# Residual stack of four layers: gating cut in two around the turns of x, low-rank transpose between the two chunk products

## The reference, cut to what matters

```
x = x + L0(x)   # masked long convolution per sequence h, kernel from 64 complex states: irfft(rfft(u) * rfft(k)), plus u * D
x = x + L1(x)   # x @ W1.T + 2 * sum over 8 experts of gate * (x @ A_e.T) @ B_e.T, 16 ranks each
                # gate: softmax of the top 2 of (x @ Wr.T + language bias)
x = x + L2(x)   # x @ W2.T + 0.5 * (x @ A_labeler) @ B.T, 32 ranks, A chosen by the label of the row
x = x + L3(x)   # x @ w_eff.T, w_eff quantized by a codebook, plus a low-rank delta
```

## Time and profile before

| what | value |
|---|---|
| median of 3 runs | 1117.43 us |
| the profiled execution | 1117.58 us, of it span 1115.8 us |
| PE busy | 1028.8 us (92% of the span) |
| PE weight load busy | 811.9 us (73%) |
| DVE busy | 851.0 us (76%) |
| ACT busy | 427.3 us (38%) |
| POOL busy | 286.8 us (26%) |
| HBM | 67 GB/s over the span |

### The profile page before, as it was taken

The page is one execution under the profiler, slowest core; times in us unless marked ns, Lnnn a source line. Parts: engine busy times, 40 slices in busy tenths (PEclk is TensorE's granted clock), DMA queues, the critical chain, the costliest instruction groups (busy, mean ns, idle before and its releaser), DMA issues.

```text
span 1115.8 us, 16634 instructions
## 1 busy us (share of the span) xinstructions
PE 1028.8 (92%) x4851; PEld 811.9 (73%) x4851; DVE 851.0 (76%) x1679; ACT 427.3 (38%) x851; POOL 286.8 (26%) x318
## 2 busy tenths in 40 slices
PE   3999999999979489999999999999999999999997
PEld 2545556988868378787788778877887788778785
DVE  5797988898970568877887788778877787778762
ACT  3222222222454344354434444444444444544431
POOL 1200340374342422321132113211321123112200
PEclk9999999999989689999999999999999999999999
DMA  9501010100003244534454445434543454344311
GB/s 249 146 20 57 19 38 1 38 1 1 1 1 50 36 69 87 99 69 76 81 99 73 73 81 100 76 69 82 100 79 66 85 96 83 66 85 89 71 38 38
DMA packets 317019, 74.95 MB, mean 67 GB/s; under 512 B 292979, under 2 KB 309555, under 8 KB 316987
## 3 DMA queue, kind: packets, MB, share of 16 engines
q1 hardware_dynamic: 316986, 74.56, 34.1%
HBM read 57.61 MB, written 16.91 MB: 67 GB/s over the span
## 4 chain that ended last, share of the span: by engine, by line
DVE 27%; issue 15%; PE 13%; ACT 9%; DVEq 1%; SPq 1%; ACTq 1%; DMA 0%
DVE ZZ L1388 7%; ACT SK L1251 5%; DVE ZZ L1379 5%; PE bank L1114 4%; DVE xT L1399 3%; PE bank L1142 3%; DVE Sl L1393 3%; PE bank L1123 2%; DVE xT L1353 2%; ACT xh L1221 2%; ACT O L1284 1%; PE bank L1169 1%; DVE low L1448 1%; PE bank L1132 1%; PE bank L1158 1%
## 5 line engine op out<-in xcount | busy, mean ns | idle before, releaser
L1068 POOL TENSOR_TENSOR Cl<-QC,Ch 128x256 fp32r<-128x256 f32 x32 | 29.7, 928 | 517.6 <-ACT Ch L1233 517.6
L1142 PE MATMUL bank<-Mh,x0l 128*128 128x512 f32 x512 | 160.9, 396 | 0.0
L1142 PE MATMUL bank<-Ml,x0h 128*128 128x512 f32 x512 | 160.5, 395 | 0.0
L1142 PE MATMUL bank<-Mh,x0h 128*128 128x512 f32 x512 | 160.3, 394 | 0.0
L1251 ACT ACTIVATE SK<-ZZ 64x448 f32<-64x448 f32 x128 | 73.8, 577 | 207.2 <-DVE ZZ L1388 204.8
L530 PE MATMUL bank<-E,A 128*128 128x512 f32 (+1 forms) x384 | 129.8, 499 | 0.0
L1388 DVE SCALAR_TENSOR_TENSOR ZZ<-ZZ,coef 128x192 f32<-128x192 f32 (+1 forms) x256 | 121.8, 516 | 10.1 <-DVE ZZ L1379 0.2
L1142 PEld LDWEIGHTS bank<-Mh,x0l 128*128 128x128 f32 x512 | 96.2, 188 | 22.9
L1142 PEld LDWEIGHTS bank<-Ml,x0h 128*128 128x128 f32 x512 | 96.2, 188 | 22.6
L530 PEld LDWEIGHTS bank<-E,A 128*128 128x128 f32 x384 | 65.6, 197 | 64.0 <-issue 64.0
L1142 PEld LDWEIGHTS bank<-Mh,x0h 128*128 128x128 f32 x512 | 94.6, 188 | 18.5
(11 more groups left out here) (283 smaller groups left out, 2022.9 us busy)
## 6 DMA issues: line engine op xcount, KB each, us to landing
X<-in_x SPq DMA_DIRECT2D x256, 64.0 KB, 2.4
XT<-in_x SPq DMA_DIRECT2D x256, 64.0 KB, 2.3
out_x<-O SPq DMA_DIRECT2D x64, 256.0 KB, 3.2
toep<-kpad SPq DMA_DIRECT2D x128, 64.0 KB, 2.2
E<-in_L_cond_W SPq DMA_DIRECT2D x8, 512.0 KB, 6.7
W2s<-in_L_cond_W SPq DMA_DIRECT2D x8, 512.0 KB, 4.3
vq<-in_L_cond_weight SPq DMA_DIRECT2D x8, 512.0 KB, 3.4
LA<-in_L_cond_lora_A SPq DMA_DIRECT2D x8, 80.0 KB, 3.4
```

Source lines behind the costliest of these rows:

```text
L1142: pe.matmul(psO[nh][:, :], xs[:, c, :], ms[:, c, nh * BANK:(nh + 1) * BANK], start=(c == 0 and n == 0), stop=False)
```

## The change

Three edits, one on each of three engines:

- VectorE: `gate` is cut in two. The first part (logits, top 2, gap, indices) stays where it was; the second part (all that needs the exponential) comes behind the two turns `turn_T(i+1)`.
- ScalarE: `gate_exp(i)` stands between the state copies of the first head and those of the second, instead of behind all copies and `s_hi`. `b_hi(i+3)` comes behind `low_hi(i)`.
- TensorE: `state_transpose(i+3)` moves from behind `gated_transpose(i)` to behind `low_transpose(i)`, and both stand between `within(i+2, 0)` and `within(i+2, 1)`.

```
--- before.py
+++ after.py
@@ -1177,16 +1177,17 @@
                         chunk_states(i + 2, 1)
                     main(i, range(NC // 2, NC))
                     gated_transpose(i)
-                    if next3:
-                        state_transpose(i + 3)
                     if next1:
                         from_states(i + 1, 0)
                         from_states(i + 1, 1)
                     low_gated(i)
                     gated_out(i)
-                    low_transpose(i)
                     if next2:
                         within(i + 2, 0)
+                    low_transpose(i)
+                    if next3:
+                        state_transpose(i + 3)
+                    if next2:
                         within(i + 2, 1)
                     low_out(i)
 
@@ -1242,11 +1243,11 @@
                             act.activation(ZZ[hh * N:(hh + 1) * N, :, ri, :], psZ[hh][ri * N:(ri + 1) * N, 0:SB].rearrange("p (c b) -> p c b", b=B),
                                            ACT.Copy).then_inc(z_out, 1)
 
-                def states_out(i, first=False):
+                def states_out(i, heads, first=False):
                     act.wait_ge(scan_step, SCAN_STEPS * (i + 1))
                     if not first:
                         act.wait_ge(sl_done, i)
-                    for hh in range(HB):
+                    for hh in heads:
                         for ri in range(2):
                             act.activation(SK[ri * N:(ri + 1) * N, hh, :].rearrange("p (c b) -> p c b", b=B), ZZ[hh * N:(hh + 1) * N, :, ri, :],
                                            ACT.Copy).then_inc(sk_done, 1)
@@ -1291,18 +1292,20 @@
                             x_hi(i + 2, hh)
                     if next1:
                         c_hi(i + 1)
-                        states_out(i + 1)
+                        states_out(i + 1, (0,))
+                    gate_exp(i)
+                    if next1:
+                        states_out(i + 1, (1,))
                         s_hi(i + 1)
-                    gate_exp(i)
                     if next2:
                         states_in(i + 2)
                     gated_hi(i)
                     if next1:
                         x0_hi(i + 1, 0)
                         x0_hi(i + 1, 1)
+                    low_hi(i)
                     if next3:
                         b_hi(i + 3)
-                    low_hi(i)
 
 
                 act.sem_inc(out_taken, 1)
@@ -1314,7 +1317,7 @@
                 for hh in range(HB):
                     x_hi(1, hh)
                 b_hi(1)
-                states_out(0, first=True)
+                states_out(0, range(HB), first=True)
                 s_hi(0, first=True)
                 x0_hi(0, 0)
                 x0_hi(0, 1)
@@ -1404,11 +1407,11 @@
                     cols = slice(hh * B, (hh + 1) * B)
                     dve.tensor_tensor(x0l[:, :, cols], xT[:, :, cols], x0h[:, :, cols].bitcast(F32), ALU.subtract).then_inc(x0l_done, 1)
 
-                GATE_STEPS = 10
-
-                def gate(i):
-
-                    done = [0]
+                GATE_STEPS, GATE_EARLY = 10, 4
+
+                def gate(i, part):
+
+                    done = [(0, GATE_EARLY)[part]]
 
                     def step(ins):
                         done[0] += 1
@@ -1417,13 +1420,16 @@
 
                     logit, top, gap, e, g0, g1, g = (gsm[:, k, :] for k in range(7))
                     w = gsm[:, 7, :]
-                    dve.wait_ge(lr_done, i + 1)
-                    step(dve.tensor_tensor(logit, psL[:, ER:ER + E], langbias[:, :], ALU.add))
-                    hold(dve, "dve")
-                    step(dve.max(top, logit))
-                    dve.tensor_tensor(gap[:, 0:1], top[:, 1:2], top[:, 0:1], ALU.subtract).then_inc(gap_done, 1)
-                    step(dve.max_index(gidx[:, :], top, logit))
-                    step(dve.tensor_copy(top[:, 0:2], gidx[:, 0:2]))
+                    if part == 0:
+                        dve.wait_ge(lr_done, i + 1)
+                        step(dve.tensor_tensor(logit, psL[:, ER:ER + E], langbias[:, :], ALU.add))
+                        hold(dve, "dve")
+                        step(dve.max(top, logit))
+                        dve.tensor_tensor(gap[:, 0:1], top[:, 1:2], top[:, 0:1], ALU.subtract).then_inc(gap_done, 1)
+                        step(dve.max_index(gidx[:, :], top, logit))
+                        step(dve.tensor_copy(top[:, 0:2], gidx[:, 0:2]))
+                        assert done[0] == GATE_EARLY
+                        return
                     dve.wait_ge(gexp_done, i + 1)
                     step(dve.tensor_scalar(w[:, 2:3], e[:, 0:1], 1.0, None, ALU.add))
                     step(dve.reciprocal(w[:, 0:1], w[:, 2:3]))
@@ -1479,10 +1485,12 @@
                         carry_across(i + 1, 2)
                         carry(i + 1, 3)
                         carry_across(i + 1, 3)
-                    gate(i)
+                    gate(i, 0)
                     if next1:
                         turn_T(i + 1, 0)
                         turn_T(i + 1, 1)
+                    gate(i, 1)
+                    if next1:
                         s_lo(i + 1)
                     gated_lo(i)
                     if next1:
```

## The result

The changed kernel takes 1075.24 us (median of 4 runs, 1073.91 to 1076.87) against 1116.66 us (4 runs of the kernel before beside it): ratio 0.963, 95% interval 0.961 to 0.965. Forecast were 1078.0, and 1073 to 1088 as the range. The profiled execution took 1073.91 us, its span 1072.1.

The account below looks back on a forecast made before the run. TensorE was taken as the bound, with holes from waits. Tiles of 21.14 instead of 22.46 save 1.32 us 28 times, 37.0, plus 2.6 in the first: 1117.58 − 39.6 = 1078.0 us, range 1073 to 1088.

Parts of the forecast that it names:

- The hole before `from_states`: On TensorE, 1.08 us a tile lost waiting for VectorE's Sl; claimed to close whole.
- the margin of Sl: VectorE's Sl, done 1.18 us after the gated transpose, would be done about 1.2 us before it.
- The surplus buys nothing: Sl done 2.48 us earlier closes the 1.08 us hole before `from_states`; being earlier than needed gains nothing more.
- The hole before the low-rank transpose: On TensorE, 0.28 us a tile between the last `gated_out` pair and L1158; claimed to close too.
- G to O: TensorE, start of gated transpose (L1147) to start of `low_out` (L1169): 6.32 us before, forecast 5.0.
- the lower end: G to O of 4.87 us, set by VectorE reaching low_lo only after x0l; time 1074.4 us.
- O to the next G: TensorE, start of `low_out` to the next gated transpose: 16.14 us, nothing waits there, taken as unchanged.
- by TensorE alone 4.96: G to O from TensorE's work only: 6.32 less the holes of 1.08 and 0.28 us.
- The exposed low-rank chain: Rival: `low_out` waits for ScalarE's lowTs, G to O 5.30, 1086.4 us; chance 0.14.
- The wait for hgTl: Rival: ScalarE's queue runs late, `low_gated` waits and half the gain goes, 1098 us; chance 0.05.
- the lower clock: Rival: TensorE's granted clock falls in the loop; 50 us of work at the lower level give 1128; chance 0.04.
- transposes that cost more than 0.11 each: Rival: state transposes cost the skill page's about 275 ns each, `low_out` at G+5.29, 1086 us; chance 0.02.

Follow-up runs that it names:

- states_only: Also cited as 3: kernel before, with only the state transposes moved behind the first chunk product and b_hi behind low_hi; 1117.39 us, ratio 1.001.
- 6: Whole change, but the second part of the gating stands ahead of the turns again, exponential still early; 1074.52 us, ratio 0.963 to the kernel before.
- 5: Whole change, but the exponential stands again behind all state copies and Sh; 1084.17 us, ratio 0.971 to the kernel before.
- lolo_early: As lolo_swap, with the low-rank transpose between second and third product of the first chunk product; 1070.73 us, ratio 0.958 to the kernel before.
- lolo_swap: Whole change, but VectorE's low_lo stands ahead of the low part of x of the second head; 1077.52 us, ratio 0.965 to the kernel before.
- 2: Kernel before, with TensorE's new order alone and b_hi behind low_hi, gating and exponential as before; 1125.77 us, ratio 1.009.
- 8: Whole change, but the low-rank transpose stands ahead of both chunk products; 1083.60 us, ratio 0.970 to the kernel before.
- 1: Kernel before, with the edits on VectorE and ScalarE alone, TensorE in its old order; 1083.69 us, ratio 0.971.

## Why the prediction was right

**Size.** Forecast was a tile of 21.14 and a gain of 37.0 us in 28 tiles plus 2.6 in the first. Measured are 21.12 a tile, 38.4 us in the 28 tiles (the kernel before takes 22.48 in the mean, not 22.46) and 2.1 in the first, where `from_states` keeps 0.3 us of its hole. From the first gated transpose to the last, the kernel before takes 693.01 us (413.02 to 1106.03) and the one after 652.52 (409.82 to 1062.34): 40.5 us. The other 3.2 us by which the two profiled spans differ stand ahead of the first gated transpose; in `states_only`, whose gating is that of the kernel before, it also comes early (410.66), so most of this is probably the execution and not the change.

**The hole before `from_states`.** Right: it closes whole, VectorE waits for hgTh instead, and the margin of Sl is 0.96 us (1.2 forecast). The difference is the 0.28 us by which VectorE's turn of x now starts later behind low_lo; from the CAST's end to Sl's end it takes 4.26 us, as forecast (4.21). "The surplus buys nothing" holds for the split (6): either order of turns and gating does. It does not hold for the exponential (5): without its early place the two engines meet with nothing to spare, and 0.22 us a tile return.

**The hole before the low-rank transpose, and `low_out`.** Right in sum, mis-sized in its parts: G to O is 4.87, the lower end, not 5.0; O to the next G is 16.24, not 16.14. The two errors cancel, and that the tile came out within 0.02 us is luck. `low_out` starts right behind low_lo, its weights can't be loaded before, and its pair keeps TensorE 0.57 us instead of 0.48. So 0.1 to 0.2 us a tile are still a wait for VectorE; `lolo_early` shows it, whose tiles are 0.15 shorter. The term "by TensorE alone 4.96" was too large: without a wait TensorE reaches `low_out` at +4.78 (`lolo_swap`). The sum had left in the low-rank transpose at the 0.29 us that it took behind its wait (643.45 to 645.12, less six products of 0.23), and it takes 0.11 without one (625.09 to 625.20).

**What the prediction missed.** It took TensorE for the bound and its waits for holes, and let the moved low-rank transpose cost nothing on VectorE. In fact the tile was VectorE's round: from the end of low_lo to the end of Sl 17.53 us (622.45, one tile of 22.46 before 644.91, to 639.98), 0.15 to `from_states`, 4.78 from there to the end of low_lo, in sum 22.46. Such a sum gives the tile whatever sets it; what makes it the bound is that in the 17.53 VectorE has one wait only, the 2.66 for the exponential (which itself stands behind copies that wait for VectorE), and that lengthening it by 0.28 lengthened the tile by 0.25 (2), while without the gap the length was as before (3). While `from_states` waits for Sl, a new order on TensorE gains nothing and can lose. The forecast still came out right because the other two edits shorten this round by more (21.11 a tile now holds 1.58 us of waiting for TensorE), so that the 0.28 us are hidden.

**The rivals.** The exposed low-rank chain did not come: the wait before `low_out` is for low_lo, but low_lo waits behind x0l, and starts at +4.54 even where the low-rank transpose stands 0.39 earlier (8). The chain that holds it begins at `from_states`, as the prediction's own lower end of 4.87 has it. The wait for hgTl, the lower clock (1.00 throughout the loop) and transposes that cost more than 0.11 each did not come either.

## What to carry to other kernels

When two in-order engines hand work to each other in a ring, add up the ring of each before pricing a hole: the chain of waits names the engine whose ring sets the time, and edits on the other are worth nothing, or less, until it is shortened. Edits then count together and not in sum: here −32 us (two engines), +10 us (the third) and −41 us for all three. On VectorE a wait at the end of a loop body cost time of its own when the loop's branch stood behind it. Holding two tiles in the loop took half of that away. In `lolo_swap`, where x0l stands behind low_lo at the end of the body, the turn of x (606.86) follows without a gap.

## What the hardware showed that was not expected

- In VectorE's loop the first instruction of the next round starts about 0.77 us after the last awaited result (lowTs done at 624.40, the turn of x at 625.17), even when the instruction that waited for it takes only 0.28: 0.28 us of idle issue a tile. With two tiles in the loop it was there in every second tile only, though the result came as late in the other. Only VectorE was measured.
- On TensorE a product whose weights are the awaited operand cost its wait twice: 0.1 us before `low_out`, and 0.10 more for its pair (0.57 in the whole change and in 2 and 5, 0.46 to 0.47 in 1, 8 and `lolo_early`, where the weights were there in time).
